# Masked cross-attention of a two-layer Perceiver: 1024-column exps, evictions and sums shared out anew over ScalarE, VectorE and GpSimd, a third bank for turned scores

## What is computed

```python
qh = (q @ Wq.T).reshape(B, Sq, H, d).transpose(0, 2, 1, 3)      # B 4, Sq 128, H 16, d 32
kh = (k @ Wk.T).reshape(B, -1, H, d).transpose(0, 2, 1, 3)      # 2048 keys
vh = (v @ Wv.T).reshape(B, -1, H, d).transpose(0, 2, 1, 3)
scores = jnp.einsum('bhqd,bhkd->bhqk', qh, kh)
scores = jnp.where(mask[:, None, :, :], jnp.float32(-1000000000.0), scores) * scale
attn = jax.nn.softmax(scores, axis=-1)
out = jnp.einsum('bhqk,bhkd->bhqd', attn, vh)
out = out.transpose(0, 2, 1, 3).reshape(B, Sq, Hd)
return out @ Wo.T
```

## Time and profile before

| | us |
|---|---|
| median of 3 runs | 1695.58 (1691.04 to 1697.31) |
| profiled execution | 1694.49 |
| span of its core's instructions | 1693.2 |
| PE busy in the span | 1628.3 (96%) |
| VectorE busy | 1065.9 (63%) |
| ScalarE busy | 908.3 (54%) |
| GpSimd busy | 126.1 (7%) |
| mean granted TensorE clock | 0.992 |

### The profile page before, as it was taken

The page is one execution under the profiler, slowest core; times in us unless marked ns, Lnnn a source line. Parts: engine busy times, 40 slices in busy tenths (PEclk is TensorE's granted clock), DMA queues, the critical chain, the costliest instruction groups (busy, mean ns, idle before and its releaser), DMA issues.

```text
span 1693.2 us, 29865 instructions
## 1 busy us (share of the span) xinstructions
PE 1628.3 (96%) x11374; PEld 1305.7 (77%) x11374; DVE 1065.9 (63%) x2282; ACT 908.3 (54%) x1910; POOL 126.1 (7%) x75
## 2 busy tenths in 40 slices
PE   7999999998999999999999999999899988999998
PEld 5778888887878878989888888877555557777776
DVE  5777777685563424565656665699534437687865
ACT  6666766663144313545545554588323335676764
POOL 0000000000000002000100010000011102233223
PEclk9999999999999999999999999999999998999999
DMA  6332323222840269988868886789730044787852
GB/s 234 125 104 82 101 80 99 88 67 90 312 147 1 74 202 303 301 246 257 269 210 257 250 264 213 228 229 260 289 136 7 7 171 171 260 321 285 291 179 77
DMA packets 147260, 308.56 MB, mean 182 GB/s; under 512 B 11452, under 2 KB 101564, under 8 KB 135548
## 3 DMA queue, kind: packets, MB, share of 16 engines
q1 hardware_dynamic: 145564, 301.65, 55.1%
q0 software_dynamic: 1536, 4.76, 0.9%
HBM read 225.16 MB, written 81.22 MB: 181 GB/s over the span
## 4 chain that ended last, share of the span: by engine, by line
PE 84%; DVE 6%; ACT 4%; DMA 2%; issue 2%; DVEq 1%; SPq 0%; POOL 0%; ACTq 0%; POOLq 0%
PE bank L128 15%; PE bank L130 14%; PE bank L129 14%; PE bank L1306 6%; PE bank L1684 4%; PE bank L1328 3%; PE bank L2215 3%; PE bank L1296 3%; PE bank L2219 2%; PE bank L2216 2%; PE bank L2250 2%; PE bank L1783 2%; PE bank L1339 2%; ACT T L1834 1%; DVE WS L2532 1%
## 5 line engine op out<-in xcount | busy, mean ns | idle before, releaser
L1374 ACT ACTIVATE TT<-TT,MX 128x512 f32<-128x512 f32 x256 | 183.6, 722 | 2.5 <-DVE MX L1433 2.5
L2532 DVE TENSOR_TENSOR WS<-EW,WS 128x1024 fp32r<-128x1024 f32 (+1 forms) x120 | 147.9, 1243 | 57.3 <-ACT WS L2363 56.5
L1427 DVE CUSTOM_DVE_ANT_0 TT<-bank,MASK 128x512 f32<-128x512 f32 x256 | 174.1, 684 | 5.6 <-PE bank L1296 3.7
L2363 ACT CAST WS<-EW 128x1024 fp32r<-128x1024 f32 (+1 forms) x144 | 139.1, 977 | 50.9 <-PE bank L2219 49.5
L1306 PE MATMUL bank<-IDN,TT 128*128 128x128 f32 x1024 | 155.4, 275 | 4.6 <-DVE PT L1440 2.5
L128 PE MATMUL bank<-BCH,WKT 128*128 128x256 f32 x512 | 150.5, 294 | 3.7 <-DVE BCL L360 3.7
L1306 PEld LDWEIGHTS bank<-IDN,TT 128*128 128x128 f32 x1024 | 120.3, 140 | 36.9 <-issue 13.0
L130 PE MATMUL bank<-BCH,WKT 128*128 128x256 f32 x512 | 145.6, 284 | 0.0
L129 PE MATMUL bank<-BCL,WKT 128*128 128x256 f32 x512 | 145.5, 284 | 0.0
L335 ACT CAST EKH<-bank 128x512 fp32r<-128x512 f32 x64 | 37.4, 585 | 148.2 <-PE bank L130 138.7
L1440 DVE COPY PT<-bank 128x512 f32<-128x512 f32 x128 | 88.1, 688 | 43.6 <-PE bank L1306 43.6
(11 more groups left out here) (335 smaller groups left out, 3779.6 us busy)
## 6 DMA issues: line engine op xcount, KB each, us to landing
EW<-in_ewg SPq DMA_DIRECT2D x48, 1024.0 KB, 5.7
KST<-tmp_k SPq DMA_DIRECT2D x43, 768.0 KB, 6.2
tmp_k<-EKH SPq DMA_DIRECT2D x128, 256.0 KB, 3.3
EW<-in_ewg SPq DMA_DIRECT2D x24, 768.0 KB, 4.9
CT<-in_ctxT SPq DMA_DIRECT2D x32, 512.0 KB, 3.5
CN<-in_ctxN SPq DMA_DIRECT2D x32, 512.0 KB, 3.6
BCT<-in_ctxT SPq DMA_DIRECT2D x32, 512.0 KB, 4.5
tmp_k<-EKL SPq DMA_DIRECT2D x64, 256.0 KB, 3.1
```

Of the source, the lines that this page charges most:

```text
L1374: act.activation(TT[:, n % 4, cs], TT[:, n % 4, cs], ACT.Exp, bias=MX[:, n % 4, 5:6], scale=SC1, accum_out=SUM[:, b % 2, h, kc:kc + 1]).th ...
L1427: dve.tensor_tensor_reduce(TT[:, sl, 512 * kc:512 * kc + 512], bank[(0, 1, 4)[g % 3]][:], MASK[:, b % 2, 512 * kc:512 * kc + 512], 1.0, NE ...
L2363: act.copy(WS[:, i % NR, 0, 0:n * w], EW[q % NE][:, at:at + n * w]).then_inc(*w_high.up)
L2532: dve.tensor_tensor(WS[:, i % NR, 1, 0:n * w], EW[q % NE][:, at:at + n * w], f(WS[:, i % NR, 0, 0:n * w]), ALU.subtract).then_inc(*w_low.up)
```

## The change

- An exp covers two quarters, 1024 columns (`exp`, at even steps only); SUM holds two partial sums per head in place of four.
- Evictions of turned scores: ScalarE takes three of four, VectorE those with g % 4 == 3. Both do the eviction of turn g - 1 in step g, so a step behind PE's turn.
- A third bank, 3, joins the ring for turns once the background is over; values then always use bank 7.
- VectorE keeps the reduction and reciprocal of the sums; the product with the identity goes to GpSimd, whose mask conversions 2 and 3 come after pairs 7 and 15.
- The copy and scaling of a pair's result come two steps later in the loops (`value(g - 4)`), and the projection of a pair is planned two steps later (`g - 4`, `g - 3`).

```diff
@@ cross_plan
-                    if len(waiting) < 8:
+                    if len(waiting) < 8 or waiting[7][1] > g - 3:
...
-                    if waiting[0][1] > g - 2:
+                    if waiting[0][1] > g - 4:
...
-                    turn_bank[g] = 5 + turns % 2
+                    ring = (5, 6) if left > 0 else (5, 6, 3)
+                    turn_bank[g] = ring[turns % len(ring)]
...
-                        value_bank[v // 8] = 7 if left > 0 or v // 8 % 2 else 3
+                        value_bank[v // 8] = 7
@@ p_kept, cross_pe
-            return (p_dve if g % 2 else p_act)[g // 2]
+            return p_dve[g // 4] if g % 4 == 3 else p_act[g - g // 4]
...
-                if pc % 2 == 0:
-                    pe.wait_ge(*s_exp[4 * (2 * p + 1) + pc // 2])
+                if pc % 4 == 0:
+                    pe.wait_ge(*s_exp[2 * (2 * p + 1) + pc // 4])
@@ cross_act
-                b, h, cs = n // 16, n % 16, slice(512 * kc, 512 * kc + 512)
-                if kc == 0:
-                    act.wait_ge(*s_max[n])
-                act.activation(TT[:, n % 4, cs], TT[:, n % 4, cs], ACT.Exp, bias=MX[:, n % 4, 5:6], scale=SC1,
-                               accum_out=SUM[:, b % 2, h, kc:kc + 1]).then_inc(*s_exp.up)
+                if kc % 2 == 0:
+                    b, h, cs = n // 16, n % 16, slice(512 * kc, 512 * kc + 1024)
+                    if kc == 0:
+                        act.wait_ge(*s_max[n])
+                    act.activation(TT[:, n % 4, cs], TT[:, n % 4, cs], ACT.Exp, bias=MX[:, n % 4, 5:6], scale=SC1,
+                                   accum_out=SUM[:, b % 2, h, kc // 2:kc // 2 + 1]).then_inc(*s_exp.up)
 
             def turn(g):
-                if g % 2 == 0:
+                if g % 4 != 3:
...
-            for g in range(256 + 2):
+            for g in range(256 + 4):
+                if 1 <= g < 256 + 1:
+                    turn(g - 1)
                 if g < 256:
-                    turn(g)
                     exp(g + 8)
...
-                    value(g - 2)
+                    if g >= 4:
+                        value(g - 4)
@@ cross_dve (its loop changes as that of cross_act)
-                if g % 2:
+                if g % 4 == 3:
...
-                own(dve.reciprocal(RS[:, c:c + 2], RS[:, c:c + 2]))
-                if p:
-                    dve.wait_ge(*sums_mm[p - 1])
-                dve.tensor_tensor(DG, IDN[:].unsqueeze(1).broadcast_to([128, 2, 128]),
-                                  RS[:, c:c + 2].unsqueeze(2).broadcast_to([128, 2, 128]),
-                                  ALU.mult).then_inc(*sums_diag.up)
+                dve.reciprocal(RS[:, c:c + 2], RS[:, c:c + 2]).then_inc(*sums_turned.up)
@@ cross_pool
+            def pair_sums(p):
+                c = 2 * (p % 8)
+                pool.wait_ge(*sums_turned[p])
+                if p:
+                    pool.wait_ge(*sums_mm[p - 1])
+                pool.tensor_tensor(DG, IDN[:].unsqueeze(1).broadcast_to([128, 2, 128]),
+                                   RS[:, c:c + 2].unsqueeze(2).broadcast_to([128, 2, 128]),
+                                   ALU.mult).then_inc(*sums_diag.up)
+
             pool.wait_ge(*xq_mm[3])
-            for b in range(4):
-                load_mask(b)
+            load_mask(0)
+            load_mask(1)
+            for p in range(32):
+                pair_sums(p)
+                if p in (7, 15):
+                    load_mask(p // 8 + 2)
```

More of the change, by code:

```diff
@@ L1139, in build @@
         MX = A("MX", [128, 4, 8])
-        SUM = A("SUM", [128, 2, 16, 4])
+        SUM = A("SUM", [128, 2, 16, 2])
         RS = A("RS", [128, 16])
@@ L1256, in build @@
         sums_mm, wo_mm = S.new("pe", 32), S.new("pe", 32)
-        s_exp, p_act, o_kept = S.new("act", 256), S.new("act", 128), S.new("act", 32)
+        s_exp, p_act, o_kept = S.new("act", 128), S.new("act", 192), S.new("act", 32)
         cross_root = S.new("act", 3)
-        s_masked, s_max, p_dve = S.new("dve", 256), S.new("dve", 64), S.new("dve", 128)
-        sums_diag, o_scaled, x_added, cross_var = S.new("dve", 32), S.new("dve", 32), S.new("dve", 4), S.new("dve", 3)
-        mask_made = S.new("pool", 4)
+        s_masked, s_max, p_dve = S.new("dve", 256), S.new("dve", 64), S.new("dve", 64)
+        sums_turned, o_scaled, x_added, cross_var = S.new("dve", 32), S.new("dve", 32), S.new("dve", 4), S.new("dve", 3)
+        mask_made, sums_diag = S.new("pool", 4), S.new("pool", 32)
         ld_qs, ld_vg = ([S.keep("ld", 16) for _ in range(2)] for _ in range(2))
@@ L1443, in pair_sums @@
                 b, c = p // 8, 2 * (p % 8)
-                dve.wait_ge(*s_exp[4 * (2 * p + 1) + 3])
+                dve.wait_ge(*s_exp[2 * (2 * p + 1) + 1])
                 own(dve.tensor_reduce(RS[:, c:c + 2], SUM[:, b % 2, c:c + 2, :], AX.X, ALU.add))
-                own(dve.reciprocal(RS[:, c:c + 2], RS[:, c:c + 2]))
-                if p:
-                    dve.wait_ge(*sums_mm[p - 1])
-                dve.tensor_tensor(DG, IDN[:].unsqueeze(1).broadcast_to([128, 2, 128]),
-                                  RS[:, c:c + 2].unsqueeze(2).broadcast_to([128, 2, 128]),
-                                  ALU.mult).then_inc(*sums_diag.up)
+                dve.reciprocal(RS[:, c:c + 2], RS[:, c:c + 2]).then_inc(*sums_turned.up)
             def value(g):
```

## The result

| | before | after |
|---|---|---|
| median of 5 runs, us | 1695.58 (1691.04 to 1698.08) | 1703.26 (1702.30 to 1705.68) |
| profiled execution / span, us | 1694.49 / 1693.2 | 1703.18 / 1701.4 |
| PE busy | 1628.3 (96%) | 1631.8 (96%) |
| VectorE busy | 1065.9 (63%) | 1018.8 (60%) |
| ScalarE busy | 908.3 (54%) | 901.0 (53%) |

The ratio after to before is 1.0052 with a 95% interval of [1.0032, 1.0072]: slower by half a per cent, though VectorE and ScalarE have less to do. Between the medians lie 7.7 us.

What follows compares the result with a forecast made beforehand. PE bounds the first regime and VectorE the second; a loop of waits (+2.1), late evictions (+2.7) and a shorter key wait (-1.2) sum to +3.6 us, about 1699 us, range 1686 to 1707.

Steps and rivals of the forecast that it cites:

- my sum: Whole kernel: the terms +2.1, +2.7, -1.2 and 0 give +3.6 us, about 1699 us against the runs shown.
- Second regime, the loop of 9.63: About 1099 to 1184 us: waits through maximum, long exps and evictions make the period 9.63 for 9.40, +2.1 us.
- First rival, the sums rule: Second regime: relieved VectorE lets PE run 8.7 us periods; net 1691, or 1684 if key wait and low clock vanish; chance 0.32.
- First regime, +2.7: Background projection, 660 to 1090 us: turns wait for VectorE's eviction at step 3, 0.18 us in each of 15 pairs.
- Other evictions have over 0.5 us to spare: First regime: evictions other than that of turn 3 delay no turn, so they were priced at nothing.
- my sign against me: Sign that the forecast is wrong: PE waits beyond 6 us in total before 1090 us.
- the second rival: First regime: turns wait on evictions behind background work, 0.7 us per pair over 20 pairs, +14 us, 1710; chance 0.13.
- Diagonal on GpSimd, 0: Product with the identity on GpSimd: about 0.8 us, hidden since PE needs it a whole period later; cost 0.
- Later scaling, 0: Scaling and projection two steps later: scaled rows ready about when PE's step 5 wants them; cost 0.
- my upper bound: Later scaling: at worst 0.3 us per period.
- End of the regime, -1.2: Last key transfer: slower periods take 1.2 us off PE's 2.60 us wait; between 0 and 5 possible.

Runs made afterwards that it cites:

- e1: Changed kernel with each eviction back in its turn's step, ahead of the exp, on both engines: 1694.53 us, ratio 0.9998.
- e2: Changed kernel with 512-column exps and four partial sums again, evictions still a step behind: 1697.9 us (single).
- e4: Kernel before with only the evictions a step behind the turn, on ScalarE and VectorE: 1729.9 us (single).
- e7: Kernel before with 1024-column exps and nothing else: 1690.9 us (single).
- e6: Changed kernel with evictions in the turn's step, and scaling and projection where the kernel before had them: 1691.3 us (single).
- e9: e6 with the next block's weights requested from step 232, every second step, in place of from 205, every fifth: 1684.89 us, ratio 0.9931.
- e5: Changed kernel with evictions in the turn's own step and the output projection planned two steps later: 1696.2 us (single).
- e10: The kernel of e6 again, timed twelve times against the kernel before: 1699.3 us, ratio 1.0001.
- e8: Changed kernel, evictions still a step behind, with only the output projection planned two steps later: 1703.2 us (single).
- e12: Kernel before with only the requests for the next block's weights moved, as in e9: 1692.91 us, ratio 0.9978.

## Why the prediction held, and where its terms did not

The forecast of 1699 and its range of 1686 to 1707 hold the 1703.26, and "within 0.5%" was the likeliest class; by the medians the difference is 0.45%, by the ratio 0.52%, on that bound. The slowdown, 7.7 us, is about twice the 3.6 of my sum.

- **Second regime, the loop of 9.63:** right, link by link; 9.61 measured. The exp I took at 1.14 keeps ScalarE 1.14 to 1.15 us. ScalarE is busy 7.94 us in a period, not 7.6. The loop cost 1.15 us over eight periods and not 1.8, because one of the eight periods of before was 9.94 and their mean 9.47. In that one VectorE adds a batch's projection to X, which takes 0.59 us from it:

```profile
1134.77 0.68 DVE L1465 TENSOR_TENSOR X<-X,bank 128x512 f32<-128x512 f32 x1
...
1135.36 0.68 DVE L1427 CUSTOM_DVE_ANT_0 TT<-bank,MASK 128x512 f32<-128x512 f32 x1
```

  Where VectorE is the bound, that makes the period 0.54 longer; in the changed kernel the period with the same addition is 9.62. That the loop closes through the evictions' place is shown by e1, that the exps lie in it by e2's 0.15 us; e4 shows the cost of late evictions on VectorE. That long exps are harmless where VectorE is the bound is shown by e7.
- **First rival, the sums rule:** refuted for this change, and true of what stood behind it. With the loop opened and the scaling early, PE runs at 8.81 (e6, e9) where the sums gave 8.7. Its other part, that faster periods only sharpen the key wait, is shown by e5 and e10.
- **First regime, +2.7:** the step that failed is "Other evictions have over 0.5 us to spare". The 0.18 per pair was right (0.17), but it was the only place that I priced. The projection of eight pairs also takes a bank of the ring, and it costs 1.6 us each of two times; the last pair loses 1.1, of which 0.87 at the turn behind the copy of values, and e1 takes that back too (18.36). 6.3 in all. By the distances of the spreads 5.2 of them lie before the last pair, so my sign against me, waits beyond 6 us before 1090, was just missed and not met. In kind this is the second rival, at places that I hadn't worked out and at under half its price.
- **Diagonal on GpSimd, 0:** right. It takes 0.61 us (0.8 taken) and nothing waits for it. The row that follows shows that GpSimd idles nearly a whole period for it:

```profile
1156.79 0.61 POOL L1507 TENSOR_TENSOR YT<-IDN,RS 128x256 f32<-128x256 f32 x1 [8.99 <-PE bank L1322]
```

- **Later scaling, 0:** right in the changed kernel, by grace of the longer loop: in one of eight periods PE waits 0.22 us for it (the row at 1151.82 below), in the others only a weight load does. As a property of the step it was wrong: without the loop it is worth 9.44 - 8.81 = 0.63 us a period, twice my upper bound.

```profile
1151.82 1.10 PE L1340 MATMUL bank<-WO,YT 128*128 128x512 f32 x2 [0.22 <-DVE YT L1456]
```

- **End of the regime, -1.2:** -3.1, within its bounds, but that is luck. PE's key wait went from 2.60 to 2.1 us, and the stretch after it had a granted clock of 1.00 where it had been 0.53. The higher clock isn't the change's doing as far as the runs show: e7, with the periods of before and a wait of 2.5 us, kept 1.00 as well, and took 26.33 us for the three pairs, 3.3 less than the kernel before.

```profile
1196.00:1202.00 6.00, 5.39 (x94) 4.29 (x93) 3.67 (x12) 3.28 (x6) 0.62 (x1) 1.00 0.50 179
```

The sum of my terms, +3.6, stands against +4.1 in the account by pieces (without the start and the rest). That closeness is luck too: the first regime, 3.6 too low, and the two other terms, 1.0 and 1.9 too high, nearly cancel. Without the last three pairs my terms give +4.8 and the pieces +7.2: the first regime makes that gap, and the loop, taken 1.0 too high, narrows it.

The Trainium skill (page "Perfetto Trace Analysis", section "Optimizing Scalar/DVE Operations") says that breaking instructions up can help where an engine causes bubbles without being full. e2 agrees, by 0.15 us a period. Putting the evictions ahead of the long exps and the scaling back, which that section doesn't speak of, was worth 0.80 (9.61 to 8.81).

**Open:** the 0.12 of e8, what the three-to-one split of evictions and the diagonal on GpSimd are worth each by itself, and what lowers the granted clock in the program's rest, which its scatter follows.

## What to carry to other kernels

When no engine is full, add up the longest loop through in-order queues and bank rings, and list every user of a ring, not only the regular one. An instruction that frees a bank belongs ahead of the long instruction in its engine's order; a third bank hides a misplaced one but doesn't pay for it. Each wait that is removed promotes the next (VectorE's load at 9.4 us a period, the misplaced eviction at 9.6, the scaling at 9.4, then the key transfers at 8.8), so follow the chain to its end before you judge a version. And take a second profile of the same kernel before you lay a difference of a few us to a change: here two of one kernel differed by 9 us in the stretch where the keys come late.

## What the runs showed of the hardware beyond what I expected

- A 1024-column exp keeps ScalarE 1.14 to 1.15 us where two of 512 columns take 0.71 to 0.72 each: 0.28 us saved per pair of them, and ScalarE's busy time fell from 64.31 to 55.87 us in 75 (e7 and before, above).
- The last key transfer took 15.4 us to land in e10, with the next block's weights requested from step 205, and 9.4 in e9, with them from step 232. In the kernel before it took 12.5 us, in e12 5.8.
- The length of PE's wait for keys didn't by itself decide whether the granted clock fell behind it. After 2.60 us it was 0.53 for 6 us in the kernel before, and after 1.60 us it was 0.72 for 6 us in e6; after 2.64 us (e1), 2.49 (e7) and 2.08 (the changed kernel) it was 1.00. The windows of 6 us behind the waits of e1 and e6:

```profile
1188.00:1194.00 6.00, 5.40 (x96) 4.49 (x95) 3.36 (x10) 2.94 (x6) 0.61 (x1) 1.00 0.45 155
```

```profile
1171.00:1177.00 6.00, 6.00 (x89) 5.00 (x88) 2.14 (x6) 2.23 (x6) 0.61 (x1) 0.72 1.06 251
```
